# Attention order: each head does its first and then its second half of the tokens, where all heads did first halves and then second halves

## What is computed

```python
# NH, NKV, HD = 16, 4, 128; b, s = 2, 1024
q = (x @ Wq.T).reshape(b, s, NH, HD); k = (x @ Wk.T).reshape(b, s, NKV, HD); v = (x @ Wv.T)...
q = q * cos + rotate_half(q) * sin            # RoPE, k likewise
scores = einsum('bqhd,bkhd->bhqk', q, repeat(k, 4)) / sqrt(HD)
scores = where(causal, scores, min)
out = einsum('bhqk,bkhd->bqhd', softmax(scores), repeat(v, 4)).reshape(b, s, NH * HD) @ Wo.T
x = layernorm(x + out)
x = layernorm(x + moe(x))                     # 64 experts, top 6, and a shared one
```

## Time and profile before

| | |
|---|---|
| median of three runs | 1486.67 us |
| profiled execution | 1487.81 us, span 1486.0 us |
| busy, share of the span | TensorE 86%, its weight load 77%, VectorE 71%, ScalarE 57%, GpSimd 47% |
| attention | from 0 to about 946 us |
| TensorE busy from 40 to 920 us | 820.86 of 880.00 us |
| VectorE busy from 40 to 920 us | 649.23 of 880.00 us |
| granted TensorE clock | mean 0.949 over the span, 0.99 from 40 to 920 us |

### The profile page before, as it was taken

How to read it: one execution, slowest core, us unless ns; L and a number is a source line. 1 busy time by engine, 2 the same in 40 slices (tenths; PEclk the granted TensorE clock), 3 DMA queues, 4 the chain that set the end, 5 groups by cost and what they waited for, 6 DMA issues and landing times. The chain is left out here.

```text
span 1486.0 us, 28187 instructions
## 1 busy us (share of the span) xinstructions
PE 1281.2 (86%) x8956; PEld 1142.2 (77%) x8956; DVE 1049.8 (71%) x2092; ACT 842.0 (57%) x1859; POOL 704.9 (47%) x718
## 2 busy tenths in 40 slices
PE   4899899899999899899899989745971999999966
PEld 3789788788889789789789879644641999999954
DVE  3677777677777777777777777665210999999956
ACT  2565565555565565565555555371211899999932
POOL 3442543433443433443443341007774788888840
PEclk9999999999999999999999999757985999999979
DMA  6320050120041120032210000104223888888868
GB/s 221 104 73 1 2 155 22 54 73 1 1 136 42 54 68 7 1 118 61 67 50 1 1 1 2 33 1 93 103 103 115 248 266 261 263 259 263 268 206 271
DMA packets 100293, 151.29 MB, mean 102 GB/s; under 512 B 10410, under 2 KB 73038, under 8 KB 100196
## 3 DMA queue, kind: packets, MB, share of 16 engines
q1 hardware_dynamic: 89156, 124.75, 27.7%
q0 software_dynamic: 11040, 25.30, 5.0%
HBM read 92.51 MB, written 62.46 MB: 104 GB/s over the span
## 5 line engine op out<-in xcount | busy, mean ns | idle before, releaser
L476 DVE TENSOR_REDUCE neg_max<-scores 128x1 f32<-128x256 f32 (+7 forms) x256 | 192.8, 753 | 197.2 <-PE scores L587 197.2
L394 ACT ACTIVATE pt_hi<-pt 128x512 fp32r<-128x512 f32 (+3 forms) x384 | 174.7, 490 | 245.5 <-PE pt L596 244.4
L515 PE MATMUL o_ps<-pt_hi,v_hi 128*128 128x256 f32 (+1 forms) x640 | 194.5, 304 | 25.5 <-DVE o_lo L452 23.7
L444 DVE TENSOR_TENSOR pt_lo<-pt,pt_hi 128x512 fp32r<-128x512 f32 (+3 forms) x384 | 201.5, 553 | 19.8 <-ACT pt_hi L394 14.0
L371 ACT ACTIVATE probs<-scores,neg_max 128x256 f32<-128x256 f32 (+7 forms) x256 | 190.1, 743 | 32.1 <-DVE neg_max L476 31.5
L333 POOL TENSOR_TENSOR turned<-taken,cos 128x512 f32<-128x512 f32 x80 | 107.6, 1346 | 167.1 <-ACT taken L381 166.9
L596 PE MATMUL pt<-ident,probs 128*128 128x128 f32 x1152 | 169.6, 274 | 18.0 <-DVE pt_lo L444 9.6
L516 PE MATMUL o_ps<-pt_lo,v_hi 128*128 128x256 f32 (+1 forms) x640 | 180.5, 282 | 0.0
L517 PE MATMUL o_ps<-pt_hi,v_lo 128*128 128x256 f32 (+1 forms) x640 | 180.0, 281 | 0.0
L325 POOL TENSOR_TENSOR q_lo<-turned,q_hi 128x512 fp32r<-128x512 f32 x64 | 83.2, 1300 | 184.1 <-ACT q_hi L404 184.1
L336 POOL TENSOR_TENSOR turned<-turned,turn_sin 128x512 f32<-128x512 f32 x80 | 102.3, 1279 | 132.6 <-DVE turn_sin L485 132.6
(11 more groups left out here) (189 smaller groups left out, 3706.2 us busy)
## 6 DMA issues: line engine op xcount, KB each, us to landing
rows_dram<-empty SPq DMA_DIRECT2D x32, 919.1 KB
up_raw<-in_up SPq DMA_DIRECT2D x69, 368.0 KB
x_in<-rows_dram SPq DMA_DIRECT2D x68, 258.0 KB, 3.3
parts<-results_dram SPq DMA_DIRECT2D x16, 768.0 KB, 9.6
down_raw<-in_down SPq DMA_DIRECT2D x69, 128.0 KB
down_raw<-in_down_tail SPq DMA_DIRECT2D x69, 112.0 KB
w_raw<-in_w SPq DMA_DIRECT2D x8, 768.0 KB, 9.1
x_raw<-in_xT SPq DMA_DIRECT2D x8, 512.0 KB, 4.8
```

The costliest lines, as they stand in the source:

```text
L394: nc.scalar.activation(pt_hi[m // 2 % 2][:, a:z, P * (m % 2):P * (m % 2) + P], pt_ps[c % 2][:, 0:P * (z - a)].rearrange("p (k q) -> p k q" ...
L444: nc.vector.tensor_tensor(pt_lo[m // 2 % 2][part], pt_ps[c % 2][:, 0:P * (z - a)].rearrange("p (k q) -> p k q", q=P), pt_hi[m // 2 % 2][pa ...
L476: nc.vector.tensor_reduce(neg_max[:, n % 4:n % 4 + 1], scores_ps[n % 2][:, score_cols(n)], AX.X, ALU.max, negate=True).then_inc(max_made, 1)
L515: nc.tensor.matmul(out, lh, rh, start=first, stop=False)
```

## The change

Within a kv head the order of the quads becomes head 0 first half, head 0 second half, head 1 first half, and so on; before it was heads 0 to 3 first half, then heads 0 to 3 second half. `key_tiles`, the head and half of a Q fill, the head of an O fill and the row tile of its addition follow from that. Both halves of K and V are now needed by the second quad, so their fills move to -9, -5 (K0, K1) and -1, 3 (V0, V1), and the waits for V's lower part with them. The splits of x move from steps -20 and -4 to -13 and -9 (the last Q that reads a half of x is now one of the last two), which puts both behind the first weight split at -16, and the second is now in the loop order before the copy of the K0 fill. Number and size of all instructions stay.

```diff
--- before.py
+++ after.py
@@ -73,20 +73,20 @@
 FIRST = 7
 SPLITS = 2
 
-FILLS = {"K": [16 * i - 9 for i in range(2 * KV_ROUND)],
-         "V": [16 * i - 5 for i in range(2 * KV_ROUND)],
+FILLS = {"K": [32 * (i // 2) + 4 * (i % 2) - 9 for i in range(2 * KV_ROUND)],
+         "V": [32 * (i // 2) + 4 * (i % 2) - 1 for i in range(2 * KV_ROUND)],
          "Q": [4 * q - 6 for q in range(QUADS)],
          "O": [4 * (i // 2) + 8 + i % 2 for i in range(2 * QUADS)]}
 ROPES = sorted([("K", i) for i in range(2 * KV_ROUND)] + [("Q", i) for i in range(QUADS)],
                key=lambda use: FILLS[use[0]][use[1]])
-SPLIT_X = [-20, -4]
+SPLIT_X = [-13, -9]
 SPLIT_W = [-16, 16]
 SPLIT_WO = [2, 34]
 
 
 def key_tiles(n):
 
-    return 4 * (n // 16 % 2) + n % 4 + 1
+    return 4 * (n // 4 % 2) + n % 4 + 1
 
 
 def chunks(n):
@@ -217,12 +217,12 @@
 
         def w_cols(kind, i):
 
-            head = {"K": GROUP, "V": GROUP + 1}.get(kind, i % GROUP)
+            head = {"K": GROUP, "V": GROUP + 1}.get(kind, i // 2 % GROUP)
             return slice(head * HD, (head + 1) * HD)
 
         def half(kind, i):
 
-            return i // GROUP % 2 if kind == "Q" else i % 2
+            return i % 2
 
         def kv_of(kind, i):
 
@@ -406,7 +406,7 @@
                     i = at(SPLIT_X, n)
                     if runs(i, SPLITS, first, last):
                         act.wait_ge(x_in, 16 * (SPLITS * k + i + 1))
-                        act.wait_ge(filled["rope"], now(k, len(ROPES), rope_of("Q", 12 + 4 * (i % 2) - 1 + QUADS * (i // 2 - 1)) + 1))
+                        act.wait_ge(filled["rope"], now(k, len(ROPES), rope_of("Q", QUADS - 2 + i % 2 + QUADS * (i // 2 - 1)) + 1))
                         nc.scalar.activation(x_hi[:, :, i % 2 * HALF:(i % 2 + 1) * HALF], x_raw[:], ACT.Copy).then_inc(x_hi_made, 1)
                     i = at(SPLIT_W, n)
                     if runs(i, SPLITS, first, last):
@@ -463,7 +463,7 @@
                         dve.wait_ge(filled["O"], now(k, per("O"), use[1] + 1))
                         dve.wait_ge(inv_made, now(k, QUADS, use[1] // 2 + 1))
                         for t in range(2):
-                            tile = 4 * (i // 8 % 2) + 2 * (i % 2) + t
+                            tile = 4 * (i // 2 % 2) + 2 * (i % 2) + t
                             col = 4 * (i // 2 % 4) + 2 * (i % 2) + t
                             row = resid[:].rearrange("p i c -> p (i c)")[:, bass.ds(k // (NKV // KV_ROUND) * (BT * H) + tile * H, H)]
                             ins = nc.vector.scalar_tensor_tensor(out=row, in0=proj_ps[:, t * H:(t + 1) * H],
@@ -538,7 +538,7 @@
                     if kind == "O":
 
                         q, a = i // 2, i % 2
-                        u, head = q // 8 % 2, q % GROUP
+                        u, head = q // 8 % 2, q // 2 % GROUP
                         pe.wait_ge(o_split, now(k, PAIRS, i + 1))
                         if q % 8 == 0 and a == 0:
                             pe.wait_ge(wo_split, now(k, SPLITS, q // 8 + 1))
@@ -601,8 +601,8 @@
 
                         u, count = j // 16 % 2, key_tiles(2 * j + 1)
                         if n % 2 == 0:
-                            if j % 8 == 0:
-                                pe.wait_ge(v_split, now(k, per("V"), j // 8 + 1))
+                            if j % 16 in (0, 2):
+                                pe.wait_ge(v_split, now(k, per("V"), 2 * (j // 16) + j % 16 // 2 + 1))
                             pe.wait_ge(pt_split, now(k, CHUNKS, chunks_before(2 * j + 2)))
                             pe.wait_ge(o_split, now(k, PAIRS, j))
                         for t in (range(count // 2) if n % 2 == 0 else range(count // 2, count)):
```

## The result

The changed kernel takes 1496.22 us (median of 6 runs, 1494.38 to 1500.36), the kernel before in the same runs 1487.08; the ratio is 1.0064, interval 1.0052 to 1.0077: slower by 9 us or 0.6%, which is clear of the runs' noise. The profiled execution has a span 9.1 us longer.

What follows compares the result with a forecast made beforehand. TensorE bounds the kernel, full except idles at quad ends behind VectorE's chain. From 1487.81 us: loop -0.7, start +4, x +1, clock -4.7 + 8.8 give 1496.2, or 1495 against the median; range 1476 to 1510.

Steps and rivals of the forecast that it cites:

- Length of a quad from VectorE's chain: Plain quad ends: maximum, turn_sin, pt_lo, o_lo set the length; 13.82 and 12.81 us, TensorE idle 1.84 and 0.40.
- Fills: Quads with K or V fills in the loop: V0 14.66, K0 14.8, V1 15.9, K1 14.8 us; head 113.4.
- Clock: Loop: falls behind the 1.70 us idles go, -4.7 us; 5.6 falls behind the 1.84 idles come, +8.8.
- The rival in which the clock stays up: Loop: the 1.84 us idles never bring the clock down; 1486 us against the median, chance 0.23.
- the one in which every idle brings it down: Loop: each of 15 idles of 1.84 us costs a fall, 23.6 us and not 8.8; 1510 us, chance 0.12.
- Splits of x: Second half of x split beside the K0 rope, x_hi 1.06 us on ScalarE: +1 us in all rounds, bounds 0 to 4.
- Start: Before the loop: K0's copy +3 us, first score +8, of which some comes back; +4 us net, bounds 1 and 9.
- no lower clock would stand behind a K fill: Loop sign: windows of 0.88 clock stand behind some of the 1.84 us idles, none behind a K fill.
- The bound of 115 us per head: Loop sign: the prediction is wrong if a head takes under 112 or over 115 us.
- loop, start and last head: Steady loop -0.7 us and start +4 us; nothing at the end, routing and experts.

Runs made afterwards that it cites:

- before_sin_late: Kernel before with the two turn_sin products one step later on VectorE: 1495.14 us, ratio 1.006.
- alt_late2: Changed kernel with the second split of x at step -7, turn_sin one step later and v_lo ahead of it: 1461.67 us, ratio 0.9826.
- pad: Changed kernel with 14 unread matmuls added in TensorE's 1.84 us idle at the end of each kv head's two plain heavy quads: 1487.93 us, ratio 1.0002.
- x_late: Changed kernel with the second split of x at step -7 instead of -9, behind the K0 rope: 1494.36 us, ratio 1.0043.
- pad_x_late: Changed kernel with the second split of x at step -7 and the 14 unread matmuls in the 1.84 us idles: 1477.94 us, ratio 0.9933.
- before_late2: Kernel before with turn_sin one step later on VectorE and the v_lo block ahead of it: 1475.37 us, ratio 0.9919.
- before_x: Kernel before with only the splits of x moved to steps -13 and -9, as in the change: 1491.32 us, ratio 1.0022.
- alt_late2_fh: Changed kernel, second x split at -7, turn_sin later behind v_lo, each round's second-head K and V fills at heavy quads' ends: 1459.90 us, ratio 0.9817.

## Why the prediction was right, point by point

The slower time and its main mechanism (VectorE's chain, the 1.84 us of idle, the falls behind it) came out as forecast. That the sum came within some 1 us is luck: two of its terms were off by 10 us each, in opposite directions.

- Length of a quad from VectorE's chain: 13.82 and 12.81 forecast, 13.82 and 12.81 measured; idle 1.84 and 0.40 forecast, 1.84 and 0.41 measured. before_sin_late and alt_late2 show that the chain sets it: without turn_sin the plain quads of before_sin_late are all shorter, and the plain pair of alt_late2 is 25.14 us, not 26.63.
- Fills: V0 14.66 forecast, 14.48 measured; V1 15.9 and 15.96; K0 14.8 and 14.68; K1 14.8 and 14.32 (idle 0.53 where I took 1.0). The head came to 112.7 and not 113.4, so the loop gained 0.8 us per head, some 5 us in all, where I had 0.7 in all.
- Clock: 5.6 falls forecast at the 1.84 (+8.8 us), 7 in the profiled execution, 1.53 us each: 10.7, 2 more than forecast. As a net of runs, pad gives 8.3 us. The rival in which the clock stays up is refuted, and so is the one in which every idle brings it down: it was 7 of 17, and 9 of 17 in x_late. Which of the idles do it was not settled, but they come in pairs: over these two traces the second 1.84 of a head has a fall in 7 of the 8 heads in which the first has one, and in 1 of the other 8. So 3 in 8, taken over from the 1.70, was a rate that happened to fit. The rule of thumb in the Trainium skill (TensorE: Matmul & The Clock Gate, section "HAM oscillation — how this bites in real kernels") warns only of waits longer than these; it misses the falls that these runs show.
- Splits of x: this term failed. I had +1 us in all, bounded at 4, from x_hi on ScalarE. It was 3 x 3.69 = 11.1 us in the profiled execution: 2.09 of each from idle, the rest from a fall of the clock. I moved the step and counted the instruction of ScalarE, not that of GpSimd: x_lo (2.40 us) stands before the K rope's product with cos, and the two turn_sin go from 1.60 + 0.69 us beside that product alone (347.24 us) to 2.72 + 1.66, 2.09 more. The x_hi that I had counted cost nothing here: the first turn_sin starts 4.25 us behind the mark with the split and 4.26 without.
- Start: first score +6.9 (forecast +8), K0's copy +1.2 (forecast +3, since the load, issued at 12.05, was there by 15.67, 3.6 us and not 4.8). The first mark is +3.3, the second head's first mark only +1.2, with a fall behind a 1.84 in it. What comes back comes in the first head's second quad, which takes 12.08 us where the other heads have 15.96: V1 is filled in it too, but it has half the output products and no output projection of an earlier head, and TensorE is busy all through it. In the kernel before, the second quad had 10.96 in the other heads and 10.00 here, with a fall in it. The K1 fill, from which I had 1 to 2 us coming back, is no part of this: the first head still has four fills (V1, and K0, K1 and V0 of the next). So the start costs next to nothing, where I had +4. The last head (its last seven quads) is 1.2 us shorter, 92.45 for 93.62.
- Signs: I had said that no lower clock would stand behind a K fill, and it stands behind the 2.77 us in all three K0 quads with the split. The bound of 115 us per head, over which I would be wrong, is passed too by the heads as they ran (116.1 us on average), since I had left the clock and the split out of the 113.4.
- Readings: the ends of the K quad of 12.23 us are in the first row of rows 6 and not the second; the longer K quads are three in eight and not one in two; and there are 17 idle times of 1.84, where I counted 15.

Up to the end of the attention the profiled execution is 10.4 us longer (947.34 to 957.74 us at the first layer norm statistics), and 1.3 us come back behind it. The forecast was +8.4. The terms: clock at plain quads 10.7 - 4.7 = +6.0 (forecast +4.1), x +11.1 (forecast +1), loop, start and last head together -6.7 (forecast +3.3). So the sum was right to about a microsecond (1495 for 1496.2) with two errors of some 10 us against each other: the split of x, put too low, and loop, start and last head, put too high. The sign rested on the clock and the split: pad_x_late, which takes away both, is on the other side.

## What to carry to other kernels

Where an in-order chain of another engine sets the length of a stage, giving the busiest engine less or more to do beside it changes only its idle time; the chain has to be shortened, and here its slow link was work for a later stage that stood at the front of the queue. When a step is moved, every engine's part of it moves, and the part on the least busy engine (here GpSimd) can be the dear one, because what stands behind it is on the path. Put extra work of the busiest engine where it is idle anyway; in pad that also kept its clock up.

## What the runs showed of the hardware

- TensorE's clock fell to 1.2 GHz (granted 0.50) behind idle times of 1.70 to 1.89 us inside dense work, at some of them and not at others: 3 of 8 behind the 1.70 of the kernel before, 7 of 17 behind the 1.84 of the changed kernel and 9 of 17 in x_late, 7 of 8 behind the 1.88 of before_late2. Behind the first head none was seen behind idles of 1.22 us or less, nor behind the 1.40 in before_x. A single idle is not all that counts, though: in the first head of alt_late2_fh the clock is at 0.50 from 56.17 to 59.58 us, behind four idles of 0.30 to 0.81 us between 51.6 and 56.0. A fall cost 1.4 to 1.6 us. Filling the idle with matmuls whose result nobody reads removed them at all 16 places that were filled (pad and pad_x_late).
- turn_sin (VectorE, both inputs in SBUF) takes 0.69 us alone and up to 2.72 beside a GpSimd instruction: the row at 227.82 ends 0.5 us after x_lo does (227.60 + 2.40). pt_lo, with one input in PSUM, is not stretched: in the changed kernel's loop one of 512 columns takes 0.68 to 0.69 us whether a GpSimd instruction runs beside it or not. The Trainium skill (SBUF — State Buffer, "Who interferes with whom") says that a VectorE instruction with two SBUF inputs contends with a GpSimd instruction that reads SBUF, and that one with at most one SBUF input, outside its 2-port modes, does not. The rows agree.
